# Moving the second unit's loads behind the last stores of a projection, and the residual and output weight loads into the loop, in a cross-attention and feed-forward kernel

## The chip, the cores and the metric

The kernel runs on one core of one Trainium2 chip. The metric is the device time in microseconds of one execution; several executions were timed and their median is given, and one further execution was profiled.

## The reference

The input x is (2, 512, 512) and the context (2, 1024, 512), in f32. The reference computes a cross-attention layer with 16 heads of 32, then a feed-forward layer, each with its residual:

```python
q = rms_norm(linear(layernorm(x), q_w, q_b), norm_q_w)
# the first 257 context rows are "image" keys, the rest "text" keys
k, v = rms_norm(linear(ctx_txt, k_w, k_b), norm_k_w), linear(ctx_txt, v_w, v_b)
k_img, v_img = rms_norm(linear(ctx_img, k_img_w, k_img_b), norm_k_img_w), linear(ctx_img, v_img_w, v_img_b)
x = x + linear(attention(q, k_img, v_img) + attention(q, k, v), o_w, o_b)
# feed-forward: only the last token is "thought" about, in 4 steps
thought = layer_norm(layernorm(x))[:, -1] @ agg_w + agg_b
for _ in range(4):
    thought += gelu(layer_norm(thought) @ d1_w + d1_b) @ d2_w + d2_b
out = layernorm(x) + sigmoid(layernorm(x) @ gate_w + gate_b) * (thought @ bc_w + bc_b)
x = x + layer_norm(out)
```

## The kernel before

One function, `make_plan`, writes out a list of steps by hand. Each engine walks through the same list and emits its own part of each step, so the list fixes the order of the instructions on TensorE, ScalarE, VectorE and GpSimd and the order of the DMAs that SyncE issues. A wait on a semaphore in one step holds up everything that stands behind it on that engine.

The work has three stages. First the projections. There are six tiles of 512 columns (`TILES`: four of keys and two of queries, in the order key, key, query, query, key, key), each of four pieces of 128 rows (`oc`). TensorE makes a piece (`proj`, L817), ScalarE adds the bias and squares, GpSimd and TensorE sum the squares (`sumsq`, L1525 and L854), and in the step `norm` VectorE scales the piece (L1332), splits it into a high part (L1336) and a low part (L1337) in one of the two buffers `hl`, and SyncE stores that buffer to DRAM (L687, `kscr` or `qscr`). A `norm` with number n first waits until the store n-2 has landed, since it writes the same buffer (the two lines `if n >= 2: dve.wait_ge(hl_stored[n % 2], ...)` between L1332 and L1336). The value projections (`v`) are stored through `vstore`.

Second the attention loop. It has 16 units (one half of the queries, one batch, one group of four heads), each of 8 steps r, so unit u is r = 8u to 8u+7. The step `S1` (L893) makes scores of one head and half of the keys with queries on the partitions, of which VectorE takes maxima (L1348, L1350); `S2` (L910) makes the scores again with keys on the partitions, ScalarE takes their exponential (L1163), `PV` multiplies with the values (L929) and adds up the sums (L934, and GpSimd's adding L1572 and L1575). S1 runs 12 steps ahead of S2 (`ahead = 8 + LEAD`), so in step r TensorE issues S1 of step r+12, and S1 of unit u begins at r = 8u-12. The first 12 steps of S1 are woven into the last key projection and the second batch's value projection. Two S1 tiles stand in PSUM banks that are freed by the maxima of tiles before.

Operands of a unit come back from DRAM on SyncE's queue: `load_k(u, half)` is three DMAs of 256 KB (L722, and for the first three units one more of 256 KB from `iscr`, L714), `load_q(u)` three of 128 KB (L739), `load_v(u)` one of 576 KB (L769), `load(u)` is `load_q(u)` and `load_k(u, 0)`. In the loop `load_k(u, 1)` stands at r = 8(u-3)+5, `load(u)` at r = 8(u-2), `load_v(u)` at r = 8(u-1)+1. The step `phase2` (L755, L756) waits on SyncE for the last value projection, for all stores of keys, queries and values and for the three `iscr` loads, and then loads six residual tiles `x2s` of 256 KB and the output weight `wbuf` of 1024 KB.

Third, beside the later units, the thin chain of the last token: its weights `d1` and `d2` come in eight pieces of 1024 KB, `late(3)` to `late(10)`, issued by GpSimd (L1591, L1594). `late(2)` clears a buffer. `bias(f)` lets GpSimd add the output bias to residual tile f (L1534); `bias(0)` first waits for all six tiles. The output projection `o(k, n)` (L968) stands at r = 38, 40, 67, 66, 101, 102, and its weight buffer is then reloaded by GpSimd with the weight of `ch_agg` (L1556, L987). `ch_d1` of the first chain step (L1005) stands at r = 77 and `ch_d2` (L1025) at r = 80.

Of the kernel before, what the change touches and what calls it, by code (L numbers as in the profile page):

```python
# [47 lines left out]
HALF_1_DONE = 1 + max(ORDER.index(c) for c in range(4, 8))  # L48
NX = 4
XS = 6  # L50
MIX_DVE = (7,)
F_AT = (110, 114, 117, 120, 124)
LEAD = 4
# [16 lines left out]
def make_plan():  # L70

    plan = []
    add = lambda *e: plan.append(e)
# [69 lines left out]
    add('late_ctx')  # L143
    add('norm', 2, 2)
    add('norm', 2, 3)
    add('load_k', 1, 1)
    add('load_k', 1, 0)
    add('load_q', 1)

    proj(4, (0,))  # L150
    add('sumsq', 3)
# [6 lines left out]
    proj(4, (3,))  # L158
    add('norm', 3, 2)
    add('norm', 3, 3)  # L160

    for oc in range(KC):
        proj(5, (oc,))
# [7 lines left out]
    for c in range(CH):  # L171
# [7 lines left out]
            add('shift', 0)  # L179
        if c == 6:  # L180
            add('spread', 0)
    add('phase2')

    ahead = 8 + LEAD
    extra, post = {}, {}
# [83 lines left out]
    def fillers(r):  # L269
        if r == 2:  # L270
            add('late', r)
        elif r % 8 == 7 and r // 8 < XS:
            add('bias', r // 8)
        elif r % 8 == 5 and r < 64:
            add('late', 3 + r // 8)
        for e in extra.get(r, []):
            plan.append(e)

# [6 lines left out]
    r = 0  # L285
    while r < 8 * NU + 2:
        t = r + ahead
        if r // 8 in PAIRED:
            add('S2', r)
            if r % 8 == 2 and r > 8:  # L290
                add('attn_log', r // 8 - 1)
            loads(r)
            maxima(t)
            maxima(t + 1)
            add('S2', r + 1)
            if r % 8 == 2 and r > 8:
                add('attn_exp', r // 8 - 1)
            loads(r + 1)
            if t % 8 == 0 and t <= 8 * NU:
                add('shift', t // 8 - 1)  # L300
                add('spread', t // 8 - 1)
            value_products(r)
            fillers(r)
            fillers(r + 1)
            if r % 8 == 4 and r > 8:
                add('weigh', r // 8 - 1)
            plan += post.get(r, []) + post.get(r + 1, [])
            r += 2
            continue
# [6 lines left out]
        if t % 8 == 0 and t // 8 <= NU:  # L316
            add('maxes', t // 8 - 1)
        fillers(r)
        if r % 8 == 1 and 8 < r < 8 * NU:
            add('weigh', r // 8 - 1)  # L320
        if t < 8 * NU:
            add('S1', t)
        if t % 8 == 1 and t <= 8 * NU + 1:
# [10 lines left out]
             ('f_stat2', 7), ('f_out', 6), ('f_out', 7)]  # L334
    plan = [e for e in plan if e[0] != 'f_mix' or e[1] in MIX_DVE]
    assert len(plan) == len(set(plan))
# [18 lines left out]

def build(nc, T, out):
    plan = make_plan()

    jobs = [e for e in plan if e[0] in JOBS and not (e[0] in ('ch_d1', 'ch_d2') and e[2] < KC - 1)
# [66 lines left out]
    def unit(u):  # L426
        k = u // NG
        return 1 - k // NB, k % NB, u % NG
# [6 lines left out]
    with ctx:  # L435
# [4 lines left out]
        def sb(name, shape, dt, off):  # L440
            return nc.alloc_sbuf_tensor_at(name, shape, dt, offset=base + int(off))
# [65 lines left out]

        x2e = sb("x2e", [P, 8 - XS, D], F32, arena)
        x2n = sb("x2n", [P, NX, D], F32, arena + 4 * KB_)
# [4 lines left out]
        bcb1 = sb("bcb1", [P, D], F32, rest + 20 * KB_ + 512)  # L514
        x2s = sb("x2s", [P, XS, D], F32, rest + 22 * KB_ + 512)

        def residual(f):
            return x2s[:, f, :] if f < XS else x2e[:, f - XS, :]

# [120 lines left out]
        def x2n_of(f):  # L640

            return (x2n_done, f + 1) if f < XS else (x2n_last, f - XS + 1)

# [4 lines left out]
        def _(sp):  # L648
# [96 lines left out]
            def phase2():  # L745
# [5 lines left out]
                for i in range(3):  # L751
                    sp.wait_ge(ind_placed[i], 16)
                for f in range(XS):
                    h, b, _ = unit(NG * (f // 2))
# [505 lines left out]
        def _(dve):  # L1260
# [30 lines left out]
            def stats(src, st, mean_var):  # L1291
                link(dve.bn_stats(st, src))
                return dve.bn_aggr(mean_var, st)
# [189 lines left out]
            def f_stat2(f):  # L1483
                if f not in MIX_DVE:
                    dve.wait_ge(mix_done, f + 1 - sum(m < f for m in MIX_DVE))
                stats(zt[:, f % NX, :], fst[:, f % 2, :], fmv[:, f % 2, :]).then_inc(f_stats, 1)
# [20 lines left out]
        def _(pool):  # L1507
# [104 lines left out]
            def f_sig(f):  # L1612
                if f in MIX_DVE:
                    return
                h, b, _ = unit(NG * (f // 2))
                z = zt[:, f % NX, :]
                pool.wait_ge(gate_done, f + 1)
                if f < 2:
                    pool.wait_ge(emptied_by['dve'], emptied(job_at[('ch_spread', 1)])[1])
                link(pool.tensor_tensor(z, z, (bcb0, bcb1)[b][:, :], ALU.mult))  # L1620
                pool.tensor_tensor(z, z, x2n[:, f % NX, :], ALU.add).then_inc(mix_done, 1)
# [39 lines left out]
```

## Time and profile before

| quantity | value |
|---|---|
| median of 3 runs | 549.47 us |
| lowest and highest | 548.84 and 552.58 us |
| profiled execution, its own time | 550.23 us |
| its span, first to last instruction | 548.4 us |
| TensorE busy | 499.8 us, 91% of the span |
| VectorE, ScalarE, GpSimd busy | 352.9, 301.9, 233.9 us |
| bytes moved by DMA | 91.92 MB, mean 168 GB/s |

The profiled execution took 550.23 us, of which 548.4 us are the span and 1.8 us lie around it. Busy shares are averages over all stages; what ends a wait in one place is read from the trace of that place.

### The profile page before, as it was taken

To read this page: it belongs to the slowest core of one execution; us is meant where nothing else is said; L and a number is where in the kernel's file an instruction comes from. 1 tells how busy PE (TensorE), PEld (TensorE's weight loads), DVE (VectorE), ACT (ScalarE), POOL (GpSimd) and SP (SyncE) were. 2 spreads that over 40 slices of the span, in tenths; PEclk is the share of its full clock that TensorE was granted. 3 is DMA by queue.
4 is the path that set the end of the run, shared out by engine and by line. 5 is a ranking of instruction groups with operands and counts; after the bars stand their busy time and mean duration, and the time that the engine had idled before them with its cause. 6 is when DMAs were issued, how large, how long until landed. Compare 5 with 4: busy or idle time off the path is not lost.

```text
span 548.4 us, 9829 instructions
## 1 busy us (share of the span) xinstructions
PE 499.8 (91%) x3768; PEld 320.9 (59%) x3768; DVE 352.9 (64%) x778; ACT 301.9 (55%) x540; POOL 233.9 (43%) x139
## 2 busy tenths in 40 slices
PE   4999999789799499999999999999999999998970
PEld 3888878567576366665666464455554455554430
DVE  4388756557866377766776587474756385348655
ACT  4874376423156366655666364757563655677432
POOL 1230024210035736675566437061625174849531
PEclk9999999979999799999999999999999999999995
DMA  8977568928698989984899487525252563000101
GB/s 295 387 243 270 188 134 279 220 76 257 251 222 289 218 231 244 225 223 116 234 221 232 82 220 176 130 59 130 59 130 59 159 164 121 2 19 23 38 19 57
DMA packets 61295, 91.92 MB, mean 168 GB/s; under 512 B 4480, under 2 KB 29072, under 8 KB 60672
## 3 DMA queue, kind: packets, MB, share of 16 engines
q1 hardware_dynamic: 56848, 74.68, 51.0%
q0 software_dynamic: 3280, 14.51, 8.0%
q10 hardware_dynamic: 1120, 2.10, 1.2%
q8 instruction: 30, 0.49, 0.4%
q14 instruction: 17, 0.14, 0.1%
HBM read 71.87 MB, written 19.66 MB: 167 GB/s over the span
## 4 chain that ended last, share of the span: by engine, by line
PE 68%; DVE 10%; DMA 9%; ACT 4%; POOL 4%; issue 2%; SPq 2%; POOLq 0%; DVEq 0%; ACTq 0%
PE psum L817 12%; PE psum L910 12%; PE psum L929 11%; PE psum L893 11%; PE psum L934 6%; PE psum L968 5%; DMA qscr<-hl 3%; PE psum L1005 3%; PE psum L1025 3%; DMA in_wki<-wki 2%; DMA qst<-qscr 2%; PE psum L1061 2%; DVE negt L1350 2%; POOL added L1575 1%; DVE negt L1348 1%
## 5 line engine op out<-in xcount | busy, mean ns | idle before, releaser
L1163 ACT ACTIVATE prob<-psum 128x512 f32<-128x512 f32 x256 | 138.9, 596 | 108.7 <-PE psum L910 86.3
L1350 DVE TENSOR_REDUCE negt<-psum 128x1 f32<-128x512 f32 (+1 forms) x256 | 133.2, 547 | 29.9 <-PE psum L893 29.7
L1575 POOL TENSOR_TENSOR added<-added,prob 128x1024 f32<-128x1024 f32 x48 | 114.6, 2388 | 11.4 <-ACT prob L1163 7.3
L893 PE MATMUL psum<-kst,qst 96*128 96x512 f32 x256 | 86.8, 434 | 18.2 <-DVE negt L1350 9.9
L910 PE MATMUL psum<-qst,kst 112*128 112x256 f32 x512 | 98.1, 308 | 1.7 <-ACT prob L1163 1.4
L910 PEld LDWEIGHTS psum<-qst,kst 112*128 112x128 f32 x512 | 77.7, 189 | 36.5 <-ACT prob L1163 17.1
L1572 POOL TENSOR_TENSOR added<-prob 128x1024 f32<-128x1024 f32 x16 | 37.9, 2370 | 137.9 <-ACT prob L1163 137.9
L929 PE MATMUL psum<-prob,vring 128*32 128x256 f32 x1152 | 84.0, 389 | 0.0
L1348 DVE TENSOR_REDUCE negt<-psum 128x1 f32<-128x257 f32 x128 | 53.0, 414 | 48.0 <-PE psum L893 47.8
L893 PEld LDWEIGHTS psum<-kst,qst 96*128 96x128 f32 x256 | 43.4, 191 | 49.2 <-DVE negt L1350 20.3
L1525 POOL TENSOR_TENSOR ssum<-sq 128x512 f32<-128x512 f32 x6 | 9.1, 1525 | 81.7 <-ACT sq L1128 64.2
L929 PEld LDWEIGHTS psum<-prob,vring 128*32 128x32 f32 x1152 | 27.9, 109 | 20.6 <-issue 0.5
L934 PE MATMUL psum<-prob,ones 128*32 128x256 f32 x512 | 36.4, 379 | 0.0
L1127 ACT ACTIVATE raw<-psum,colp 128x512 f32<-128x512 f32 (+2 forms) x32 | 19.0, 593 | 30.8 <-PE psum L817 30.3
L817 PE MATMUL psum<-p_wv,tok 128*128 128x512 f32 x144 | 34.3, 391 | 0.0
L1061 PE MATMUL psum<-wg,xTt 128*128 128x512 f32 x64 | 30.2, 608 | 0.6 <-ACT xTt L1231 0.6
L817 PEld LDWEIGHTS psum<-p_wv,tok 128*128 128x128 f32 x144 | 26.9, 188 | 5.5
L968 PE MATMUL psum<-wbuf,attT 128*128 128x512 f32 x64 | 29.4, 601 | 0.4 <-issue 0.4
L817 PE MATMUL psum<-tok,p_wk 128*128 128x256 f32 (+1 forms) x144 | 26.7, 338 | 0.0
L1145 ACT ACTIVATE vbuf<-psum 128x512 f32<-128x512 f32 x14 | 8.4, 598 | 33.2 <-PE psum L817 33.2
L817 PEld LDWEIGHTS psum<-tok,p_wk 128*128 128x128 f32 x144 | 22.7, 202 | 2.4
L817 PE MATMUL psum<-tok,p_wq 128*128 128x512 f32 x96 | 23.5, 401 | 0.0
(161 smaller groups left out, 671.6 us busy)
## 6 DMA issues: line engine op xcount, KB each, us to landing
kst<-kscr SPq DMA_DIRECT2D x96, 256.0 KB, 6.2
vring<-vscr SPq DMA_DIRECT2D x16, 576.0 KB, 5.5
kscr<-hl SPq DMA_DIRECT2D x16, 512.0 KB, 3.0
d<-d POOLq DMA_DIRECT2D x8, 1024.0 KB, 6.7
qst<-qscr SPq DMA_DIRECT2D x48, 128.0 KB, 5.2
vscr<-vbuf SPq DMA_DIRECT2D x18, 256.0 KB, 3.1
qscr<-hl SPq DMA_DIRECT2D x8, 512.0 KB, 4.6
in_c<-ctxT SPq DMA_DIRECT2D x2, 1024.0 KB, 12.7
```

The costliest lines, as they stand in the source:

```text
L817: mm = pe.matmul(ps, left(a, kc), right(b, kc), start=(kc == 0 and a + b == 0), stop=(kc == KC - 1 and a == 1))
L893: pe.matmul(psum[:, tile_bank[n], :], qst[0:96, slot, jj, qt * P:(qt + 1) * P], kst[0:96, slot, jj, half * 512:(half + 1) * 512], start=Tr ...
L910: mm = pe.matmul(score2[:, j * QH:(j + 1) * QH], kst[0:96 + 4 * HPG, slot, jj, k0:k0 + P], qst[0:96 + 4 * HPG, slot, jj, :], start=True, s ...
L929: mm = pe.matmul(psum[32 * j:32 * j + 32, PV_BANK, st * QH:(st + 1) * QH], vring[:, u % 2, vc, 32 * j:32 * j + 32], prob[:, r % NP, j * QH ...
L934: mm = pe.matmul(psum[32 * j:32 * j + 32, SUM_BANK, st * QH:(st + 1) * QH], ones[:, kind, :], source[:, j * QH:(j + 1) * QH], start=first, ...
L968: mm = pe.matmul(ps, attT[:, g, n * P:(n + 1) * P], wbuf[:, g, :], start=(g == 0), stop=(g == NG - 1))
L1061: mm = pe.matmul(ps, xTt[:, f % 2, kc, :], wg[:, kc, :], start=(kc == 0), stop=(kc == KC - 1))
L1163: act.activation(prob[:, r % NP, part], score2[:, part], ACT.Exp).then_inc(exp2_done, 1)
L1348: dve.tensor_reduce(negt[:, u % 2, qt, 0, j:j + 1], psum[:, tile_bank[n], 0:IMG], AX.X, ALU.max, negate=True)
L1350: dve.tensor_reduce(negt[:, u % 2, qt, half, HPG + j:HPG + j + 1], psum[:, tile_bank[n], k0:512], AX.X, ALU.max, negate=True)\
L1572: pool.tensor_tensor(added[:, :], prob[:, (r - 1) % NP, :], prob[:, r % NP, :], ALU.add).then_inc(added_done, 1)
L1575: pool.tensor_tensor(added[:, :], added[:, :], prob[:, r % NP, :], ALU.add).then_inc(added_done, 1)
```

## The change

Four edits, all in `make_plan`. (1) `load_k(1, 1)`, `load_k(1, 0)` and `load_q(1)` move from behind `norm(2, 3)` to behind `norm(3, 3)`. (2) `phase2` moves from ahead of the loop to r = 10. (3) The pieces of d1 and d2 move from r = 5, 13, 21, 29, 37, 45, 53, 61 to r = 21, 29, 37, 45, 53, 61, 65, 69. (4) The six `bias` steps move from r = 7, 15, 23, 31, 39, 47 to r = 23, 31, 39, 47, 55, 63.

```diff
@@ -48,6 +48,7 @@
 XS = 6
+LATE_AT = (21, 29, 37, 45, 53, 61, 65, 69)
 MIX_DVE = (7,)
@@ -143,9 +144,6 @@
     add('norm', 2, 2)
     add('norm', 2, 3)
-    add('load_k', 1, 1)
-    add('load_k', 1, 0)
-    add('load_q', 1)
 
     proj(4, (0,))
     add('sumsq', 3)
@@ -158,6 +156,9 @@
     proj(4, (3,))
     add('norm', 3, 2)
     add('norm', 3, 3)
+    add('load_k', 1, 1)
+    add('load_k', 1, 0)
+    add('load_q', 1)
 
     for oc in range(KC):
         proj(5, (oc,))
@@ -179,7 +180,6 @@
             add('spread', 0)
-    add('phase2')
 
     ahead = 8 + LEAD
@@ -269,10 +269,12 @@
         if r == 2:
             add('late', r)
-        elif r % 8 == 7 and r // 8 < XS:
-            add('bias', r // 8)
-        elif r % 8 == 5 and r < 64:
-            add('late', 3 + r // 8)
+        elif r == 10:
+            add('phase2')
+        elif r % 8 == 7 and 2 <= r // 8 < XS + 2:
+            add('bias', r // 8 - 2)
+        elif r in LATE_AT:
+            add('late', 3 + LATE_AT.index(r))
```

## Rows read from the trace of the kernel before

**Rows 1.** The page: busy times, and the granted clock in 40 slices.

```profile
PE 499.8 (91%) x3768; PEld 320.9 (59%) x3768; DVE 352.9 (64%) x778; ACT 301.9 (55%) x540; POOL 233.9 (43%) x139
...
PEclk9999999979999799999999999999999999999995
```

**Rows 2.** TensorE by time: start, us, line, tiles, [idle before <-releaser].

```profile
112.20 0.80 PE L893 MATMUL psum<-kst,qst 96*128 96x512 f32 x1 [5.19 <-DVE negt L1350]
112.79 5.32 PE L817 MATMUL psum<-tok,p_wk 128*128 128x512 f32 x12
...
119.47 2.91 PE L817 MATMUL psum<-tok,p_wk 128*128 128x512 f32 x12
```

**Rows 3.** VectorE by time, 100 to 113 us.

```profile
100.72 1.66 DVE L1337 TENSOR_TENSOR hl<-raw,hl 128x512 fp32r<-128x512 f32 x1
...
108.54 0.43 DVE L1336 CAST hl<-raw 128x512 fp32r<-128x512 f32 x1 [5.50 <-DMA qscr<-hl]
...
111.46 1.28 DVE L1350 TENSOR_REDUCE negt<-psum 128x1 f32<-128x512 f32 x2
```

**Rows 4.** The chain that ended last, 80 to 125 us.

```profile
96.17 12.27 DMA qscr<-hl
```

**Rows 5.** DMA issues at 102.4 and 109.7 us: KB, us to landing.

```profile
qscr<-hl SPq DMA_DIRECT2D x1, 512.0 KB, 7.3
...
qscr<-hl SPq DMA_DIRECT2D x1, 512.0 KB, 2.8
```

**Rows 6.** SyncE's queue by time: start, us to issue, DMAs.

```profile
90.85 0.61 SPq L714 DMA_DIRECT2D kst<-iscr  x1
...
123.88 0.36 SPq L687 DMA_DIRECT2D kscr<-hl  x1
...
164.86 3.65 SPq L755 DMA_DIRECT2D x2s<-x  x6
...
171.83 2.07 SPq L739 DMA_DIRECT2D qst<-qscr  x3
```

**Rows 7.** The chain that ended last, 165 to 215 us.

```profile
173.38 12.52 DMA qst<-qscr
```

**Rows 8.** That chain in a unit without a hole.

```profile
199.59 0.84 PE psum L910 x4
...
203.58 0.93 PE psum L893 x4
...
215.43 0.84 PE psum L910 x4
```

**Rows 9.** TensorE by time, 171 to 179 us: first S2 of r = 10.

```profile
174.89 0.91 PE L910 MATMUL psum<-qst,kst 112*128 112x256 f32 x4
```

**Rows 10.** Stretches: us, busy (x) of PE PEld DVE ACT POOL, clock, DMA, GB/s.

```profile
111.60:118.30 6.70, 6.10 (x14) 4.81 (x15) 2.34 (x4) 0.07 (x1) 0.00 (x0) 0.50 0.27 100
...
183.30:190.00 6.70, 4.06 (x22) 3.11 (x26) 3.19 (x7) 1.42 (x3) 5.88 (x4) 0.50 1.14 216
...
175.30:185.90 10.60, 3.64 (x31) 2.54 (x30) 3.32 (x12) 4.47 (x9) 9.09 (x6) 0.87 1.08 252
...
164.90:185.90 21.00, 14.04 (x152) 9.06 (x144) 9.73 (x26) 10.45 (x20) 14.36 (x9) 0.94 0.96 269
...
200.00:220.00 20.00, 20.00 (x197) 13.86 (x197) 15.38 (x44) 14.99 (x29) 15.31 (x8) 1.00 0.88 220
```

**Rows 11.** The page's DMA issues: KB each, median us to landing.

```profile
qst<-qscr SPq DMA_DIRECT2D x48, 128.0 KB, 5.2
...
wbuf<-agg POOLq DMA_DIRECT2D x1, 1024.0 KB, 8.3
```

**Rows 12.** GpSimd by time, 158 to 215 and 292 to 345 us.

```profile
176.50 1.28 POOL L1534 TENSOR_TENSOR x2s<-x2s,rows 128x512 f32<-128x512 f32 x1 [6.30 <-DMA x2s<-x]
...
313.33 0.77 POOL L1556 DMA_DIRECT2D wbuf<-agg  x1 [5.27 <-PE psum L968]
```

**Rows 13.** TensorE by time, 327 to 330 us: ch_agg.

```profile
328.21 1.08 PE L987 MATMUL psum<-wbuf,tT 128*32 128x128 f32 x32
```

## The prediction

> **What bounds the kernel now.** The page comes first [rows 1]: TensorE is busy 91% of the span, VectorE 64%, so in most places only what stops or slows TensorE counts. The row of the granted clock has two 7s among nines, in the slices that begin at 110 and 178 us. The view by stretches shows what they are: at 111.6 to 118.3 us and at 183.3 to 190.0 us the clock is 0.50, which is 1.2 GHz in place of 2.4 [rows 10]. Before each of them TensorE stood idle: 5.19 us up to 112.20 [rows 2], and in the second place until a load that was issued at 173.38 had landed 12.52 us later [rows 7]. Everywhere else the chain of waits runs through TensorE's own instructions, one behind the other [rows 8]. So there are two holes, and the question is what ends the wait in each.
>
> Hole A, read backwards. TensorE's S1 at 112.20 waits for a maximum on VectorE [rows 2]. VectorE takes it at 111.46, since its queue has norm(3, 2) and norm(3, 3) ahead of it, and norm(3, 2) stood 5.50 us for a store of `hl` [rows 3]. That store is the one of norm(3, 0): the chain has it issued at 96.17 and landing 12.27 us later [rows 4]. Ahead of it SyncE had issued unit 1's ten loads from 90.85 on [rows 6]: 4 x 256 from the first half with `iscr`, 3 x 256 and 3 x 128 KB, 2176 KB in all. A store of the same size with little ahead of it lands in 2.8 us [rows 5].
>
> Hole B. TensorE's S1 of r = 12 begins unit 3 and waits for unit 3's queries [rows 7]. SyncE issued them behind phase2 (six tiles from 164.86, then the output weight, 2560 KB) and behind unit 3's first keys, though nothing in unit 3 needs phase2 [rows 6]. One piece of d1, 1024 KB, ran beside them.
>
> **The change part by part.** Part 1, unit 1's loads behind norm(3, 3). It adds no instruction. The store of norm(3, 0) no longer waits for SyncE to issue the loads, so it goes out about 1 us earlier, near 95.2, and its landing is bounded by 2.8 us and by the 7.3 us of the store issued at 102.4, which still had most of unit 1's loads ahead of it [rows 5]: it is there between 98.0 and 102.5, before norm(3, 2) asks for it. VectorE ends norm(3, 1) at 100.72 + 1.66 = 102.38 as before [rows 3], its store now has an empty queue ahead, so 2.8 to 3.3 us: landed at 105.2 to 105.7. norm(3, 3) waits for this one. From the released cast to the first maximum of norm(3, 2) and norm(3, 3) were 111.46 - 108.54 = 2.92 us for two pieces [rows 3]; for the one that is left about half, 1.3 us. So the maxima start at 106.5 to 107.0, the first takes 0.7, and TensorE goes on at about 107.3 instead of 112.20: 4.9 us. It had stopped at 112.20 - 5.19 = 107.01, so about 0.3 us of idleness is left [rows 2]. Both falls of the clock came after idle times of over 5 us, so here it stays up. The twelve matmuls that took 5.32 us take 2.91 [rows 2], and of the whole slow stretch, with TensorE busy 6.10 us at half speed, half is given back: 3.05 us [rows 10]. Part 1: 4.9 + 3.05, say 8.0 us. Its bounds: if the store of norm(3, 1) took 7.3 us as before, it lands at 109.7, TensorE goes on at 111.6 and only 0.6 us are won; if it never mattered, 5.2 + 3.05 = 8.2. I take 8.0, since the DMAs that made 7.3 out of 2.8 are the ones moved away.
>
> What the loads are moved past: norm(3, 0) to norm(3, 3)'s stores on SyncE, and nothing on another engine. They are now issued at about 107 to 112. Queued behind them on SyncE is the store of norm(4, 0), at 123.88 before [rows 6], about 116 now. The 2176 KB, 2.23 MB, at 250 GB/s [rows 10] need some 9 us and 2 for the way, so they land at about 118 and that store near 119 to 121. norm(4, 2), the first that waits for it, comes two value pieces of 12 matmuls, 2.9 us each [rows 2], after norm(4, 0): about 122. The loads themselves are wanted by S1 of unit 1, behind the fifth value piece, some 10 us after they land. The narrower cover is 1 to 3 us wide; cost zero, and up to hole A's own 8 us if it is gone.
>
> Part 2, phase2 to r = 10. Unit 3's second-half keys are now issued when S2 of r = 4 is done, and its queries when S2 of r = 7 is done instead of 171.83 to 173.9 [rows 6], with nothing but keys ahead of them. r = 8 begins two steps of 15.84 / 8 = 1.98 us before r = 10's 174.89 [rows 8, 9], at 170.9, so that is about 169. The median query load takes 5.2 us [rows 11], so they are there at about 174.5, over 4 us before S1 of r = 12 asks at 174.89 + 3.99 = 178.9. The hole is then gone. What it costs is read from periods: a unit without a hole runs 215.43 - 199.59 = 15.84 us from r = 18 to r = 26 [rows 8], and the one before, from r = 10 to r = 18, took 199.59 - 174.89 = 24.70 us [rows 8, 9]. Part 2: 24.70 - 15.84 = 8.86 us, of which some 7 are the wait and the rest the clock.
>
> What phase2 is moved past, and who is now behind it: load_v(2) goes out before it, and behind it stand unit 4's second-half keys (3 x 256 KB) and queries (3 x 128 KB), which S1 wants at r = 20. When is that? r = 18 comes at 174.89 + 15.84 = 190.73, and S1 of the next pair 203.58 - 199.59 = 3.99 us later [rows 8]: 194.7. The queue has, from about 175, load_v(2) 576, phase2 2560, keys 768 and queries 384 KB, 4288 KB or 4.39 MB. The busy stretches moved 269 and 252 GB/s [rows 10]. With 1.7 us from the first issue, the queries land between 176.7 + 16.3 = 193.0 and 176.7 + 17.4 = 194.1. That is 0.6 to 1.7 us before they are wanted, so I take a mean cost of 0.5 us, bounds 0 and 3. The residual tiles have 576 + 1536 KB up to their end, 2.16 MB, so they land near 186, and bias(0) wants them at r = 23, near 200; GpSimd's wait of 6.30 us goes [rows 12], worth nothing, since TensorE soon stood in hole B.
>
> Against this move speaks a rule of the Trainium skill, "DMA: Bandwidth & Descriptors", section "Queues, rings and completion order": on each DMA engine the descriptors of an issuing engine's row are taken in ring order, and engines change between rows packet by packet. The trace agrees: the queries landed only after the 2560 KB issued before them [rows 6, 7]. By that rule phase2 delays unit 4 here as it delayed unit 3 before; what it delays is settled by the sum above, not by the rule. The same page's section "Bandwidth" gives 341 GB/s for 1 MB loads; by that figure, an estimate, the queries would be there at about 189.6 and the cost be nothing. The rows show less than that.
>
> Part 3, the pieces of d1 and d2. The two pieces that ran in the first two units leave the crowded stretch; this is what lets the 4.39 MB above have the whole rate (with one piece of 1.05 MB more they would land 4 us later, beyond 194.7). The first now stands at r = 21, just behind the point of need. The last two are new company for the chain's first weight: `ch_agg`'s weight is issued at 313.33 [rows 12], lands after 8.3 us [rows 11] and is read at 328.21 [rows 13], 6.6 us later. The piece at r = 65 is done before it is issued, the piece at r = 69 is issued behind it, so it costs nothing; if that piece took half of the rate, the 8.3 us would be 12.4 and still be covered. The last piece itself is wanted by ch_d2 at r = 80, eleven steps later. Bounds 0 and 2 us. Part 4, the bias steps: the same six instructions of 1.28 us in later units on an engine that is busy 15.31 of 20.00 us [rows 10, 12]; o(0, 0) at r = 38 and o(0, 1) at r = 40 want the ones at 23 and 31. Nothing.
>
> The sum: 550.23 - 8.0 - 8.86 + 0.5 = 533.9 for the profiled execution. That lies 0.76 us above the median of the runs before; I forecast 534.0 for the median.
>
> **The rivals.** (a) Phase2 opens hole B again one unit later. If the rate in that stretch is as in the half-speed stretch, 216 GB/s [rows 10], the queries land at 176.7 + 20.3 = 197.0, 2.3 us late, without a fall of the clock: 536. If it is worse and TensorE idles over 5 us, the clock falls too and 5 to 7 plus 2 us come back: 540.5 to 543, middle 542. For it speaks the margin of about 1 us; against it that the moved bytes of the measured stretches were themselves taken in part by DMAs issued later. (b) Hole A opens again at norm(4, 2) or at norm(3, 3), by the store behind unit 1's loads. Half of it comes back with 4 us, all of it with 8: 538 to 542, say 540. (c) The change doesn't do what it says, both holes being filled by other waits as long: 547 to 549. Against it, no second wait of that length stands beside them in the rows. (d) Slower than before: the move of phase2 and d1 leaves a backlog that the loop never works off, because each unit carries 9 loads of keys and queries (1920 KB), 576 KB and a piece of 1024 KB, 3.60 MB per 15.84 us or 228 GB/s. Then units 4 to 7 each wait 5 us and lose 2 more to the clock, 4 x 7 = 28 us, against 16.4 won: 562. It decides from the point where the DMA engines give under 228 GB/s. They moved 220 at a share of 0.88 [rows 10], so their room is some 12%, small but there.
>
> **How the numbers follow.** Chances: forecast 0.64, own range 531.5 to 537; (a) with a fallen clock 0.13; (b) 0.13; (c) 0.04; (d) 0.03; more won than summed, under 531.5, 0.03. Over them the range 531.5 to 542.0 leaves out (c), (d), the low end and half of (a), under 2 in 10. A measurement of this kernel can't tell less than 1%, 5.5 us, from no change. Faster by over 1% (under 544) is all but (c) and (d): 0.93, same 0.04, slower 0.03.
>
> **What the profile of the changed kernel would show.** Part 1 is right if the cast of norm(3, 2) has no idle time before it, TensorE's gap near 107 is under 1 us and the clock is 1.00 there, and wrong if a wait for `hl` of 4 us stands anywhere up to the last key norms. Part 2 is right if S1 of units 3 and 4 wait for no DMA, r = 10 to r = 18 takes 15.8 us and the clock row has no 7 in that place; a wait at L893 for `qst` near 187 us (194.7 less hole A's 8) would be rival (a). Part 3 is right if L987 waits for no DMA. The prediction would be wrong most likely by the 1 us of margin at r = 20, on a rate known to 7%.

## The result, and the profile after

The changed kernel takes 535.97 us in the median of 4 runs (535.1 to 537.95), and the kernel before 551.03 us in 4 runs beside it (548.84 to 556.34): a ratio of 0.972, with a 95% interval from 0.964 to 0.980. The profiled execution of the changed kernel took 536.66 us, span 534.8.

The page of the changed kernel first, its busy times and granted clock, which answer to [rows 1]. (Line numbers are two higher than before, L895 for L893 and so on.)

```profile
PE 498.2 (93%) x3768; PEld 319.2 (60%) x3768; DVE 352.5 (66%) x778; ACT 302.0 (56%) x540; POOL 233.8 (44%) x139
...
PEclk9999999999899999999999999999999999998995
```

All engines are as busy as before; the gain is idle time and clock. The two 7s of before are gone, and two 8s have come in other places, the slices from 134 and from 481 us.

TensorE in order of time, from 102 to 190 us (start, us, [idle before <-releaser]), for [rows 2] and [rows 9]:

```profile
107.83 0.50 PE L895 MATMUL psum<-kst,qst 96*128 96x512 f32 x1 [0.45 <-DVE negt L1352]
...
134.56 0.50 PE L895 MATMUL psum<-kst,qst 96*128 96x512 f32 x1 [2.77 <-DVE negt L1352]
134.90 4.50 PE L819 MATMUL psum<-p_wv,tok 128*128 128x512 f32 x12
...
143.34 0.51 PE L895 MATMUL psum<-kst,qst 96*128 96x512 f32 x1 [0.28 <-DVE negt L1352]
...
169.26 0.92 PE L912 MATMUL psum<-qst,kst 112*128 112x256 f32 x4
...
189.00 1.09 PE L895 MATMUL psum<-kst,qst 96*128 96x512 f32 x4
```

The S1 that had idled 5.19 us now idles 0.45 us. The first S2 of r = 10 is at 169.26, not at 174.89: 5.63 us of the gain lie before it. S1 of r = 20, at 189.00, has no idle time in brackets, so it waited for nothing. The chain that ended last has r = 18 and r = 26 at these times, for [rows 8]:

```profile
185.18 0.84 PE psum L912 x4
...
201.01 0.84 PE psum L912 x4
```

From r = 10 to r = 18, taken between the same two rows as in the forecast, it is now 15.9 us, not 24.7, so 8.8 us more are won there: 199.59 - 185.18 = 14.4 us together. From there to the last step of the loop the distance to the kernel before stays at 14.4 us. The spans differ by 13.6; the 0.8 us was lost at the end, in a slow stretch from 490.8 us that this execution had and the one of before hadn't.

VectorE in order of time, for [rows 3], and SyncE's queue, for [rows 6], of the changed kernel:

```profile
106.02 0.43 DVE L1338 CAST hl<-raw 128x512 fp32r<-128x512 f32 x1 [0.36 <-DMA qscr<-hl]
...
123.39 0.43 DVE L1338 CAST hl<-raw 128x512 fp32r<-128x512 f32 x1 [1.45 <-DMA kscr<-hl]
...
132.69 0.43 DVE L1338 CAST hl<-raw 128x512 fp32r<-128x512 f32 x1 [4.17 <-DMA kscr<-hl]
```

```profile
116.65 0.38 SPq L689 DMA_DIRECT2D kscr<-hl  x1
119.08 0.34 SPq L696 DMA_DIRECT2D vscr<-vbuf  x1
119.86 0.36 SPq L689 DMA_DIRECT2D kscr<-hl  x1
120.83 1.15 SPq L771 DMA_DIRECT2D vring<-vscr  x2
122.29 4.69 SPq L696 DMA_DIRECT2D vscr<-vbuf  x1
127.02 0.43 SPq L689 DMA_DIRECT2D kscr<-hl  x1
```

The wait of 5.50 us for a query store is gone. Further on there are waits for key stores: 1.45 us, which is new, then 4.17. The store that the second waits for is issued at 127.02 and lands 5.6 us later; ahead of it on SyncE stand the two value loads of 120.83 (1152 KB) and a value store whose issue alone took 4.69 us, to 126.98, where others take 0.3 to 0.5. The piece itself was ready at 124.5, when its low part was written. TensorE waits 2.77 us, and then its clock falls.

The kernel before had the second of these waits too, at the same norm (SyncE, VectorE, TensorE):

```profile
129.52 2.19 SPq L694 DMA_DIRECT2D vscr<-vbuf  x1
131.75 1.32 SPq L687 DMA_DIRECT2D kscr<-hl  x1
...
138.35 0.43 DVE L1336 CAST hl<-raw 128x512 fp32r<-128x512 f32 x1 [4.01 <-DMA kscr<-hl]
...
140.22 0.50 PE L893 MATMUL psum<-kst,qst 96*128 96x512 f32 x1 [1.21 <-DVE negt L1350]
```

The value store was issued 7.2 us earlier in the changed kernel (122.29, not 129.52), but the key store behind it only 4.7 us earlier (127.02, not 131.75), since the value store's issue took 2.5 us longer. Its landing took 5.6 us for 6.5, so the S1 that waits comes 5.66 us earlier than before, at 134.56 and not at 140.22.

Stretches of the changed kernel (us, busy (x) of PE, PEld, DVE, ACT, POOL, clock, DMA share, GB/s), for [rows 10]:

```profile
107.00:111.50 4.50, 4.05 (x18) 2.88 (x16) 2.57 (x5) 1.56 (x3) 0.00 (x0) 1.00 0.86 215
...
135.80:139.10 3.30, 3.30 (x9) 2.56 (x8) 3.16 (x7) 0.00 (x0) 0.00 (x0) 0.50 0.67 250
...
171.00:176.00 5.00, 5.00 (x52) 3.39 (x50) 4.93 (x15) 4.52 (x10) 4.71 (x3) 1.00 1.04 348
176.00:186.00 10.00, 10.00 (x110) 6.68 (x110) 6.51 (x16) 5.61 (x11) 3.99 (x3) 1.00 1.06 289
```

The last two rows are phase2's new place. The DMA engines moved 348 and 289 GB/s there, more than the 252 to 269 that the forecast took from [rows 10]. No run here shows why. And unit 4's second and third query loads, issued at 178.76 and 179.24, landed after 6.8 us in the median, so both by about 186.1 (the changed kernel's DMA issues in that stretch: KB each, median us to landing):

```profile
qst<-qscr SPq DMA_DIRECT2D x2, 128.0 KB, 6.8
```

### The profile page after: what moved, and what is told of

It is laid out like the page before. It is cut to its first block, busy times and chain, and to the rows that moved or that the text cites. A ratio compares the mean times of both kernels' runs of the same rounds, so it can differ in the third digit from the quotient of the medians.

```text
span 534.8 us, 9829 instructions
## 1 busy us (share of the span) xinstructions
PE 498.2 (93%) x3768; PEld 319.2 (60%) x3768; DVE 352.5 (66%) x778; ACT 302.0 (56%) x540; POOL 233.8 (44%) x139
## 4 chain that ended last, share of the span: by engine, by line
PE 70%; DVE 12%; DMA 5%; ACT 5%; POOL 4%; issue 3%; SPq 1%; POOLq 0%; DVEq 0%; ACTq 0%
PE psum L819 13%; PE psum L912 12%; PE psum L931 12%; PE psum L895 11%; PE psum L936 6%; PE psum L970 4%; PE psum L1007 3%; PE psum L1027 3%; DMA in_wki<-wki 3%; PE psum L1063 2%; DMA qscr<-hl 2%; DVE negt L1352 2%; POOL added L1577 1%; DVE negt L1350 1%; POOL zt L1622 1%
## 5 line engine op out<-in xcount | busy, mean ns | idle before, releaser
L895 PE MATMUL psum<-kst,qst 96*128 96x512 f32 x256 | 85.5, 429 | 6.5 <-DVE negt L1352 5.2
L895 PEld LDWEIGHTS psum<-kst,qst 96*128 96x128 f32 x256 | 43.0, 189 | 37.1 <-issue 16.1
L819 PE MATMUL psum<-p_wv,tok 128*128 128x512 f32 x144 | 35.9, 405 | 0.0
L819 PE MATMUL psum<-tok,p_wk 128*128 128x256 f32 (+1 forms) x144 | 24.4, 319 | 0.0
L936 PEld LDWEIGHTS psum<-prob,ones 128*32 128x32 f32 x512 | 16.9, 112 | 11.6 <-issue 0.9
```

Source lines behind the costliest of these rows:

```text
L819: mm = pe.matmul(ps, left(a, kc), right(b, kc), start=(kc == 0 and a + b == 0), stop=(kc == KC - 1 and a == 1))
L895: pe.matmul(psum[:, tile_bank[n], :], qst[0:96, slot, jj, qt * P:(qt + 1) * P], kst[0:96, slot, jj, half * 512:(half + 1) * 512], start=Tr ...
L936: mm = pe.matmul(psum[32 * j:32 * j + 32, SUM_BANK, st * QH:(st + 1) * QH], ones[:, kind, :], source[:, j * QH:(j + 1) * QH], start=first, ...
```

## The experiments

All are held against the kernel before on the same chip. "r = 10 at" is the start of the first S2 of that step in the profile, which was 174.89 before and 169.26 in the changed kernel. Times are medians, and the ratio is that of the means, so the two differ a little; the place in the profile says where the time went in one execution.

**Part 1 alone.** The three steps moved in the kernel before, nothing else:

```diff
@@ kernel before
     add('norm', 2, 3)
-    add('load_k', 1, 1)
-    add('load_k', 1, 0)
-    add('load_q', 1)
...
     add('norm', 3, 3)
+    add('load_k', 1, 1)
+    add('load_k', 1, 0)
+    add('load_q', 1)
```

> The kernel before with part 1 alone: unit 1's loads behind norm(3, 3), phase2, the bias steps and the pieces of d1 and d2 where they were. Theory (the parts act each in its own hole): S2 of r = 0 starts 5.6 us earlier than before, hole B stands unchanged with 24.7 us from r = 10 to r = 18, the time is about 5.6 us under before, ratio 0.990. Rival (part 1 only moves the stores' delay and part 2 did the rest): r = 0 starts under 2 us earlier, ratio over 0.996.

Measured: 545.96 us beside 550.8, ratio 0.989 (0.982 to 0.997). r = 10 at 168.04, 6.85 us early, and hole B as it was; TensorE by time:

```profile
133.38 0.50 PE L893 MATMUL psum<-kst,qst 96*128 96x512 f32 x1 [2.92 <-DVE negt L1350]
...
178.88 2.07 PE L893 MATMUL psum<-kst,qst 96*128 96x512 f32 x4 [6.79 <-DMA qst<-qscr]
```

So part 1 works alone. The profile also shows how far the clock differs from one execution to another. Two slow stretches of this profile:

```profile
175.10:185.20 10.10, 6.32 (x31) 4.55 (x32) 3.62 (x7) 2.48 (x4) 7.10 (x5) 0.50 1.14 220
328.70:335.40 6.70, 6.70 (x42) 3.63 (x44) 4.04 (x15) 3.63 (x6) 5.60 (x3) 0.50 0.58 161
```

The first, in hole B, was 6.8 us long before; the second lies in the thin chain's stage, where TensorE had waited for no more than 0.96 us and which had none before. It took 2.6 us of the gain. The longer one in hole B took 0.7.

**Parts 2 and 4 alone.** Phase2 and the bias steps as changed, everything else as before:

```diff
@@ kernel before
-    add('phase2')
...
-        elif r % 8 == 7 and r // 8 < XS:
-            add('bias', r // 8)
+        elif r == 10:
+            add('phase2')
+        elif r % 8 == 7 and 2 <= r // 8 < XS + 2:
+            add('bias', r // 8 - 2)
         elif r % 8 == 5 and r < 64:
             add('late', 3 + r // 8)
```

> The kernel before with phase2 at r = 10 and the bias steps later, the pieces of d1 and d2 as they were at r = 5, 13 and so on, unit 1's loads as they were. Theory (the order of SyncE's queue made hole B): unit 3's queries wait for nothing, but a piece of d1 now shares the engines before r = 20, so S1 of unit 4 waits 2 to 4 us there; gain from r = 10 on 5 to 7 us, ratio about 0.989. Rival (the order alone is enough and the margin was never needed): no wait at r = 20, gain 8.8 us, ratio 0.984.

Measured: 546.65 us in 10 runs, ratio 0.994 (0.989 to 0.998). Hole B is gone, 8.8 us are won from r = 10 to r = 18, and 4.5 us are lost again at r = 20. The 4.3 us that are left are less than the 5 to 7 expected, and the medians show the same, 4.2 us. (r = 10 itself is at 173.22: hole A stands, but cost 1.7 us less in this execution.) TensorE by time:

```profile
196.31 1.19 PE L895 MATMUL psum<-kst,qst 96*128 96x512 f32 x4 [3.19 <-DMA qst<-qscr]
```

In the chain of this kernel the wait is a query load of 13 us, as long as the one in hole B:

```profile
183.20 13.06 DMA qst<-qscr
```

The order of the queue made hole B, and with d1's pieces early the same hole comes back one unit later, smaller.

**Part 3 alone.** The pieces of d1 and d2 at their new steps, phase2 ahead of the loop:

```diff
@@ kernel before
-        elif r % 8 == 5 and r < 64:
-            add('late', 3 + r // 8)
+        elif r in LATE_AT:
+            add('late', 3 + LATE_AT.index(r))
```

> The kernel before with the pieces of d1 and d2 at r = 21 to 69 alone; phase2 stays ahead of the loop. Theory (the queue's order made hole B, the piece of d1 beside it only lengthened it): 1.05 MB less at 250 GB/s, so unit 3's queries land 3 to 4 us earlier, TensorE idles 3 to 4 us of 7, the gain is 3 to 5 us, ratio 0.993. Rival (the load of the DMA engines by d1 made it): the hole is gone, gain 8.8 us, ratio 0.984.

Measured: 550.49 us in 10 runs beside 550.8, ratio 0.996 (0.993 to 1.000). The hole is shorter but there:

```profile
181.43 2.08 PE L894 MATMUL psum<-kst,qst 96*128 96x512 f32 x4 [4.39 <-DMA qst<-qscr]
```

4.39 us for 7.00, and a slow stretch behind it as long as before, so 2.2 us are won. The theory had the size of the wait nearly right (3 to 4) and the gain too high. Moving the pieces alone is worth little.

**The pieces early again.** The changed kernel with that one branch put back:

```diff
@@ changed kernel
-        elif r in LATE_AT:
-            add('late', 3 + LATE_AT.index(r))
+        elif r % 8 == 5 and r < 64:
+            add('late', 3 + r // 8)
```

> The changed kernel with the pieces of d1 and d2 back at r = 5 to 61. Theory (spacing the pieces is what clears the queue before r = 20): S1 of unit 4 waits 2 to 4 us at r = 20, time 2 to 4 us over the changed kernel, or 5 if the clock falls. Rival (the pieces cost nothing where they were): as the changed kernel, within 1 us, and no wait for queries at L895.

Measured: 543.24 us beside 550.8, ratio 0.986 (0.981 to 0.990).

```profile
192.73 1.24 PE L895 MATMUL psum<-kst,qst 96*128 96x512 f32 x4 [3.55 <-DMA qst<-qscr]
```

3.55 us of waiting and a fall of the clock at r = 20, 5.0 us together, again behind a query load of over 13 us. It landed at 192.7, where the changed kernel's landed at 186.1. Part 3 is thus worth 5 us beside part 2 and 2 us without it.

**Without part 1.** The changed kernel with unit 1's loads back ahead of tile 4.

```diff
@@ changed kernel
     add('norm', 2, 3)
+    add('load_k', 1, 1)
+    add('load_k', 1, 0)
+    add('load_q', 1)
...
     add('norm', 3, 3)
-    add('load_k', 1, 1)
-    add('load_k', 1, 0)
-    add('load_q', 1)
```

> The changed kernel without part 1: unit 1's loads back ahead of tile 4, phase2, bias steps and pieces of d1 and d2 as changed. Theory (the parts add): hole A stands with a wait of 4 to 5 us near 107, r = 0 starts within 2 us of before, hole B is gone (15.8 us from r = 10 to r = 18) and r = 20 doesn't wait; 8.8 us under before, ratio 0.984, 5.6 us over the changed kernel. Rival (the kernels' gains overlap): under 4 us over the changed kernel.

Measured: 542.11 us beside 548.41, ratio 0.988 (0.983 to 0.993). r = 10 is at 173.91; r = 18 and everything behind it 9.8 us before the kernel before.

```profile
112.45 0.80 PE L895 MATMUL psum<-kst,qst 96*128 96x512 f32 x1 [5.31 <-DVE negt L1352]
```

Hole A stands, hole B is gone, r = 20 doesn't wait. It is 4.7 us behind the changed kernel at r = 10 (173.91 - 169.26), and 5.7 us behind the second profile of the changed kernel, below, which was taken in the same session; the medians of that session differ by 4.9. Within what executions differ, the parts add.

**The changed kernel again.** The same kernel, beside the next ones.

> The changed kernel once more, so that the next ones can be held against it on the same chip. The waits should be those of its first profile: one of 2.8 us on TensorE near 134 us, none at r = 12 or r = 20. If falls of the clock are not tied to one place but to what idles before and to when, the number and length of the slow stretches will differ from the first profile while the waits agree to 0.5 us.

Measured: 537.25 us beside 548.41, ratio 0.978 (0.973 to 0.983). TensorE and a stretch:

```profile
133.50 0.50 PE L895 MATMUL psum<-kst,qst 96*128 96x512 f32 x1 [2.80 <-DVE negt L1352]
...
138.52 0.50 PE L895 MATMUL psum<-kst,qst 96*128 96x512 f32 x1 [1.54 <-DVE negt L1352]
...
142.28 0.50 PE L895 MATMUL psum<-kst,qst 96*128 96x512 f32 x1 [0.30 <-DVE negt L1352]
```

```profile
134.50:138.00 3.50, 2.48 (x11) 1.69 (x9) 3.36 (x7) 0.60 (x1) 0.00 (x0) 1.00 0.70 262
```

The same wait of 2.8 us, and here the clock stayed at 1.00 behind it; r = 10 is at 168.16, 1.1 us earlier than in the first profile. This execution had its slow stretch in the thin chain, 6.8 us long from 320 us, which cost 2.7. So after a wait of 2.8 us the clock falls in some executions and not in others. Here the fall made no difference to the time: from the wait to the S1 shown last it is 8.78 us both with the fall (134.56 to 143.34) and without it (133.50 to 142.28). Both S1s wait for VectorE. Where the clock fell, the twelve matmuls behind the wait took 4.50 us and the next S1 had no wait; where it stayed up, they took 2.9 us and the next S1 but one waited 1.54 us.

**The value loads late.** What is left of hole A: are the stores late by the value loads or by unit 1's loads?

```diff
@@ changed kernel, the dictionary `before` of the second batch's value steps
-    0: (('norm', 4, 1), ('load_v', 0), ('load_v', 1)),
+    0: (('norm', 4, 1),),
...
-    4: (('norm', 5, 3), ('load_k', 2, 1), ('load', 2))
+    4: (('norm', 5, 3), ('load_v', 0), ('load_k', 2, 1), ('load', 2)), 5: (('load_v', 1),)
```

> The changed kernel with the first two value loads (1152 KB, at 120.8 us in its profile, right behind the store of norm(4, 1)) moved to behind norm(5, 3) and to the sixth value piece. Theory (these loads make the stores of tile 4 and 5 late, 5 to 9 us in place of 3, and so VectorE's wait of 4.17 us): the store of norm(4, 2) lands in about 3 us, TensorE's wait of 2.8 us falls to under 1.5 and the slow stretch behind it goes: 2 to 4 us faster than the changed kernel. Rival (unit 1's loads, which land at 121, are what delays the stores): the wait stays over 2 us, same time.

Measured: 536.47 us in the same session, ratio 0.978 (0.974 to 0.982): not to be told from the changed kernel's 537.25. But r = 10 is at 165.50, 2.7 us before that of the changed kernel again, and the store of norm(4, 2), which had gone out at 127.02 and taken 5.6 us, took 3.8. SyncE's queue shows the larger part, that it went out at 123.20, since the value store ahead of it was issued in 0.33 us and no longer in 4.69:

```profile
121.72 0.33 SPq L696 DMA_DIRECT2D vscr<-vbuf  x1
123.20 0.36 SPq L689 DMA_DIRECT2D kscr<-hl  x1
```

TensorE by time:

```profile
135.86 0.50 PE L895 MATMUL psum<-kst,qst 96*128 96x512 f32 x1 [1.42 <-DVE negt L1352]
...
203.49 1.19 PE L895 MATMUL psum<-kst,qst 96*128 96x512 f32 x4 [2.27 <-DMA qst<-qscr]
```

The theory holds for the wait, which fell to 1.42 us; VectorE's largest wait fell from 4.17 to 1.82. But 2.5 us of it came back at 203: the queries of unit 5 came too late, a wait that the changed kernel hasn't. The rival has a share as well: norm(4, 2) still waits 0.63 us for the store behind unit 1's loads. And the long issue has moved with the loads: a value store behind the second of them, at 146.28, took 4.95 us to issue.

**And the key stores first.** On top of the last, the order of two kinds of stores on SyncE:

```diff
@@ kernel with the value loads late, second batch's value steps
     for c in range(CH):
         v(1, (c,))
+        # the vstore steps of this piece are taken out of the plan here
         for e in before.get(c, ()):
-            add(*e)
+            if e[0] == 'norm': add(*e)
+        # and added here, then the steps of before[c] that aren't norms
```

> As the kernel with the value loads late, and in the second batch's value projection each piece's value stores stand behind the key stores of the same step on SyncE, so that the store of norm(4, 2) doesn't wait 2.5 us for ScalarE's copy of the value piece. Theory (SyncE's order adds 2 us to the store's issue): a further 0.5 to 2.5 us before r = 0, TensorE without a wait over 0.5 us from 108 to 150. Rival (the issue time doesn't matter once the loads are gone): as the kernel with the value loads late, within 0.3 us at r = 0.

Measured: 533.90 us in that session, ratio 0.973 (0.969 to 0.978); r = 10 at 163.75, 1.75 us before the last and 4.4 before the changed kernel again. TensorE had no idle time over 0.7 us between 104 and 150 us. The store that I had named, norm(4, 2)'s, went out at 123.23, as without this edit: with the value loads gone nothing had held it. What moved are the next two, of norm(4, 3) and norm(5, 0), from 128.96 and 129.44 to 126.54 and 128.39. They had stood behind value stores that waited for ScalarE. So SyncE's order held stores up, though not the one expected. The six runs lie between 531.52 and 537.07, those of the changed kernel between 534.53 and 539.90, and the intervals overlap: probably 3 us faster, not settled by its times.

It was run again, beside a kernel with one number more changed:

```diff
@@ kernel with the key stores first
-LATE_AT = (21, 29, 37, 45, 53, 61, 65, 69)
+LATE_AT = (27, 29, 37, 45, 53, 61, 65, 69)
```

> The kernel with the value loads late and the key stores first once more, beside the one with its first piece at r = 27. r = 0 starts 11 us before that of the kernel before, less up to 2 us where hole A's part of the clock differs; TensorE without a wait over 1.3 us up to r = 0; time 532 to 536.

> The kernel with the value loads late and the key stores first, with one number more: the first piece of d1 at r = 27 in place of 21. The queries of unit 5 land only 2 us before S1 of r = 28 in the changed kernel and were 2.3 us late in the kernel with the value loads late, with this piece beside them. Theory (the backlog behind phase2 is worked off only in unit 5, and the piece at r = 21 shares it): the queries of unit 5 land at least 3 us before they are wanted, no wait at r = 28 in any profile, 0 to 2 us faster. Rival (the lateness is of one DMA engine, not of the amount): the third query load still lands 4 us behind the second.

Measured beside 551.97 us: 535.27 us, ratio 0.969 (0.965 to 0.974), and with the first piece at r = 27 534.11 us, ratio 0.969 (0.965 to 0.974). The two can't be told apart by their times. r = 10 is at 164.65 and 163.66, as expected, but the waits behind it weren't. TensorE in the kernel with the key stores first (this profile is of the slowest of its six runs, 540.26 us):

```profile
186.52 1.52 PE L904 MATMUL psum<-kst,qst 96*128 96x512 f32 x4 [1.97 <-DMA qst<-qscr]
...
205.13 1.20 PE L904 MATMUL psum<-kst,qst 96*128 96x512 f32 x4 [1.28 <-DMA qst<-qscr]
...
223.68 1.19 PE L904 MATMUL psum<-kst,qst 96*128 96x512 f32 x4 [2.45 <-DMA qst<-qscr]
```

and in the one with the piece at r = 27:

```profile
184.36 1.19 PE L904 MATMUL psum<-kst,qst 96*128 96x512 f32 x4 [0.81 <-DMA qst<-qscr]
...
219.62 2.08 PE L904 MATMUL psum<-kst,qst 96*128 96x512 f32 x4 [3.33 <-DMA qst<-qscr]
```

With the loop starting 4 us earlier the query loads are on the edge in units 4, 5 and 6, and which of them is late differs by execution. The piece at r = 27 took away the wait of unit 5, as the theory said, and left a longer one in unit 6, so it isn't unit 5 alone that works a backlog off. Two pieces were now issued close together, at 199.17 and 204.64, and unit 6's queries right behind them, from 205.55 on, which speaks for the amount. For the rival stands that the third query load of unit 5 landed 5.6 us behind the second in the kernel with the key stores first (205.1 and 199.5), and 3.1 us behind in the other. Which of the two it is, the amount or one late DMA engine, stays open.

## Why the prediction was right

The forecast was 534.0 us, and the measured 535.97 lies 2.0 us above it and inside its own range. Measured beside each other the gain was 15.1 us; the forecast, from the first median of before, had 15.5.

Hole B, part 2: 8.86 us forecast, 8.8 measured, and the reason given is shown: in the kernel with phase2 moved alone the hole goes, in the one with the pieces moved alone it stays.

Part 3: named as what clears the way for r = 20, where with the piece early the queries would land 4 us later. Measured: a wait of 3.2 and 3.6 us, 4.5 and 5.0 with the clock. The 0.5 us charged for r = 20 was not paid in either profile of the changed kernel: the queries landed near 186.1 and were wanted at 189.0, a margin of about 2.9 us, not 0.6 to 1.7. Here two errors met, and that is luck: the margin was larger than forecast, and the piece made the queries not 4 but 6.6 us later (192.7 for 186.1). The rate taken, 252 to 269 GB/s, was too low; phase2's own stretch ran at 348 and 289. Rival (a) did not happen, and with one piece of d1 in the way it did. `ch_agg`'s weight took 8.3 us again and wasn't waited for.

Hole A, part 1: this is the term that was mis-sized. 8.0 us forecast, 5.6 (twice), 6.7 and 6.85 measured at r = 10 in the four profiles that have part 1 and the value loads in their old place. At its own place the working held. TensorE had come to 107 us 0.4 us later than in the kernel before. From there the S1 idles 0.45 us (forecast 0.3), which wins 4.7, and the clock gives back 2.9 (forecast 3.05), so that by 123 us 7.2 us are won. Together that is 7.6, and 7.6, 8.2 and 8.2 in the three other profiles.

The step that failed is "cost zero" for the new place of unit 1's loads, as rival (b) had said it might. The place of the first wait was named right: norm(4, 2) waits 1.45 us for the store behind unit 1's loads, which took 6.7 us. The forecast's "that store near 119 to 121" was too early, it landed at 123.3. That wait alone cost TensorE nothing: at 131.4 the 7.2 us were still there. The cost comes two norms on, at norm(5, 0), which the forecast didn't look at. The store it waits for stands behind a value store, and that one behind the two value loads. With unit 1's loads early the value store took 2.2 us to issue, in all four profiles; with them late, their issue ending 8 us ahead of the value loads' and not 32, it took 4.2 to 4.7, in all four. In each of these four 1.6 to 2.0 us of the gain are gone at the S1 behind it. With the value loads moved away the store is issued in 0.33 us, and the gain at r = 10 is 9.4 us, since most of the wait that the kernel before had there goes too.

By the prediction's own sign ("wrong if a wait for `hl` of 4 us stands anywhere up to the last key norms") part 1 would be wrong, since 4.17 us stand at norm(5, 0). The sign was badly chosen: the kernel before has 4.01 us in the same place.

The 3.05 us of clock were read from one execution. In the three other profiles in which hole A stands (parts 2 and 4 alone, part 3 alone, without part 1) TensorE idles 3.8, 4.8 and 5.3 us, the slow stretch behind is 3.4 us long and not 6.8, and r = 10 is at 173.22, 173.00 and 173.91 and not at 174.89. So the profile before was one with a costly hole A. Against the kernel without part 1 the part is worth 4.7 to 5.7 us at r = 10.

"Both falls of the clock came after idle times of over 5 us, so here it stays up" held at 107 us, but it is no rule: it was drawn from two cases, both long, and at 134 us the clock fell after 2.77 us. That fall cost nothing, since VectorE set the pace there.

So the parts add up as follows for the profiled execution: the sum gave 533.9 us and 536.66 were measured. Part 1 won 2.4 us less than summed, part 2 what was forecast, the 0.5 us at r = 20 were not paid, and 0.8 us went in a slow stretch near the end. The forecast for the median had one more slip: by its own sum and the 0.76 us between profile and median it should have been 533.1, not 534.0. And that the gain of the medians, 15.1 us, comes so near to the forecast's is in part luck: the parts were summed to 16.4, and the two profiled spans differ by 13.6.

Part 4 cost nothing that shows. Rival (d) lost its condition: from r = 18 on the changed kernel keeps its 14.4 us through all units.

## What to carry to other kernels

Where several kinds of transfers go out on one queue, look which one the next wait ends on, and let nothing be issued ahead of it that is wanted later; the same bytes ten steps later cost nothing here, and both holes were that. Having moved a block of transfers, find the next deadline behind its new place and sum the bytes up to it: here 1.05 MB more or less decided some 5 us. Look at more than the first wait behind the new place: the one that cost here came two norms later, on a queue that other loads had filled too. And count on a part of the gain to be met by the next such wait: in the kernels with the value loads late, what was won ahead of the loop brought the queries of units 4 to 6 to the edge of being late.
